# Edge stage of a graph network: the gathered rows are added on DVE instead of by an identity product on PE

## The reference

```python
def _L3_gnn_ref(h, edge_index, edge_attr, msg_w1, msg_b1, msg_w2, msg_b2, upd_w1, ...):
    src, dst = (edge_index[0], edge_index[1])
    m_in = jnp.concatenate([h[src], h[dst], edge_attr], axis=1)
    msg = jax.nn.relu(m_in @ msg_w1 + msg_b1) @ msg_w2 + msg_b2
    agg = jax.ops.segment_sum(msg, dst, num_segments=h.shape[0])
    upd_in = jnp.concatenate([h, agg], axis=1)
    upd = jax.nn.relu(upd_in @ upd_w1 + upd_b1) @ upd_w2 + upd_b2
    return h + upd
```

## Time and profile before

| | us |
|---|---|
| median of 3 runs | 3560.36 (3560.14 to 3565.21) |
| the profiled execution, its own time | 3566.42 |
| span of the profile | 3564.7 |
| mixed rounds of the edge stage, about | 2742 to 3503 |
| wide rounds | 3503 to 3548 |
| update of the nodes, the rest | 3548 to 3565 |

### The profile page before, as it was taken

The page is one execution under the profiler, slowest core; times in us unless marked ns, Lnnn a source line. Parts: engine busy times, 40 slices in busy tenths (PEclk is TensorE's granted clock), DMA queues, the critical chain, the costliest instruction groups (busy, mean ns, idle before and its releaser), DMA issues. The chain is left out here.

```text
span 3564.7 us, 82525 instructions
## 1 busy us (share of the span) xinstructions
PE 3252.6 (91%) x23698; PEld 2529.9 (71%) x23699; DVE 1620.1 (45%) x4433; ACT 1241.9 (35%) x3761; POOL 898.7 (25%) x938
## 2 busy tenths in 40 slices
PE   5988998989989989999789999999995999998988
PEld 3656666667764444444489999999884888888887
DVE  7977778889974320000544211111223443444444
ACT  6766777777751220000433222111332111111111
POOL 2000000000020000000067777000225656655550
PEclk8999999999999999999689999999997999999999
DMA  3012222333349378978044333222333434433431
GB/s 85 18 36 71 71 71 89 107 108 116 117 131 233 83 180 193 232 186 192 12 108 126 90 81 81 72 80 72 112 88 93 97 93 95 93 91 89 91 85 65
DMA packets 115781, 368.35 MB, mean 103 GB/s; under 512 B 37613, under 2 KB 54481, under 8 KB 102712
## 3 DMA queue, kind: packets, MB, share of 16 engines
q1 hardware_dynamic: 86647, 334.12, 34.0%
q0 software_dynamic: 25696, 29.21, 5.5%
q10 hardware_dynamic: 3154, 1.60, 0.2%
HBM read 278.22 MB, written 86.61 MB: 102 GB/s over the span
## 5 line engine op out<-in xcount | busy, mean ns | idle before, releaser
L2618 POOL DMA_INDIRECT edge_rows<-src_table,src_idx x432 | 460.5, 1066 | 307.0 <-DMA edge_rows<-src_table,src_idx 172.2
L2288 POOL DMA_INDIRECT slots<-lane,src_idx x352 | 342.1, 972 | 107.6 <-issue 107.6
L2828 ACT ACTIVATE edge_work<-edge_ps 128x1024 f32<-128x1024 f32 x114 | 116.7, 1023 | 702.7 <-PE edge_ps L2783 416.9
L1422 PE MATMUL prop_ps<-rows,y 125*128 125x500 f32 (+1 forms) x798 | 307.6, 545 | 15.2 <-DMA rows<-adj_rows 8.4
L781 ACT ACTIVATE build_place<-build_place,w 128x128 f32<-128x128 bf16 x690 | 265.0, 402 | 142.0 <-DVE build_place L725 101.6
L2797 PEld LDWEIGHTS edge_ps<-edge_work 128*128 128x128 f32 x2128 | 257.2, 195 | 65.7 <-issue 65.7
L851 PE MATMUL build_ps<-build_place 128*128 128x325 bf16 (+1 forms) x1380 | 299.0, 299 | 1.5 <-ACT build_place L781 0.4
L2797 PE MATMUL edge_ps<-edge_work 128*128 128x125 f32 x2128 | 266.2, 279 | 36.2 <-DVE m_agg_t L2667 36.2
L2773 PE MATMUL edge_ps<-m_store,edge_hot_t 125*128 x2128 | 272.3, 282 | 25.4 <-DVE edge_hot_t L2682 25.2
L2773 PEld LDWEIGHTS edge_ps<-m_store,edge_hot_t 125*128 125x128 f32 x2128 | 252.7, 195 | 35.8 <-issue 30.5
L1422 PEld LDWEIGHTS prop_ps<-rows,y 125*128 125x128 f32 x798 | 144.0, 192 | 176.9 <-issue 154.2
(11 more groups left out here) (462 smaller groups left out, 6205.9 us busy)
## 6 DMA issues: line engine op xcount, KB each, us to landing
rows<-adj_rows SPq DMA_DIRECT2D x62, 1367.2 KB
cnt_panels<-build_cnt SPq DMA_DIRECT2D x50, 683.6 KB
adj_rows<-rows SPq DMA_DIRECT2D x25, 1367.2 KB
n<-cnt_panels SPq DMA_DIRECT2D x40, 683.6 KB
orders_panel<-cnt_panels SPq DMA_DIRECT2D x40, 683.6 KB
edge_src_row<-slot_lanes SPq DMA_DIRECT2D x60, 250.0 KB
edge_dst_row<-slot_dst SPq DMA_DIRECT2D x60, 250.0 KB
h<-cnt_panels SPq DMA_DIRECT2D x20, 683.6 KB
```

The lines of the kernel that those rows point to most:

```text
L1422: last = pe.matmul(ps[:, c, 0:n * B], (y[0:B] if h else g.h)[:, row, 0:D], rows[slot][:, b0 * B:(b0 + n) * B], start=at == 0, stop=at == N ...
L2288: pool.indirect_dma_start(dr.slots, bass.IndirectOffsetOnAxis(ap=g.src_idx[:, j:j + 1], axis=0), g.pay[:, j, :], None).then_inc(s_scattere ...
L2618: pool.indirect_dma_start(rows[:, r % AHEAD, i, :], None, dr.table, bass.IndirectOffsetOnAxis(ap=g.src_idx[:, t:t + 1], axis=0)).then_inc( ...
L2828: a.activation(act[s], ps[:, 2 * s:2 * s + 2, :].rearrange("p b (t k) -> p (b t) k", k=D), ACT.Relu).then_inc(s_act[s], 1)
```

## The change

The identity product is left out. In its place DVE adds the gathered rows to slot 1's two banks and writes the result into `act[GATHERED]`, the messages' buffer (`join`); ACT takes the relu of that buffer in place. The last product of the edge values now ends `inputs` for a gathered group. A new semaphore `s_joined` lets ACT go on, and lets POOL reuse the buffer of the rows. ACT's loop is cut in two, one for the mixed rounds and one for the wide ones, whose work is as before.

```diff
--- before.py
+++ after.py
@@ -2523,6 +2523,7 @@
         s_free = [ph.sem(f"free{s}") for s in range(2)]
         s_pre = [ph.sem(f"pre{s}") for s in range(2)]
         s_act = [ph.sem(f"act{s}") for s in range(2)]
+        s_joined = ph.sem("joined")
         s_hot = ph.sem("hot")
         s_sum = ph.sem("sum")
         s_added = ph.sem("added")
@@ -2612,7 +2613,7 @@
                 if r:
                     pool.wait_ge(s_rows, r * (16 * GT))
                 if r >= AHEAD:
-                    pool.wait_ge(s_pre[GATHERED], r - AHEAD + 2)
+                    pool.wait_ge(s_joined, r - AHEAD + 1)
                 for i in range(GT):
                     t = SORTED + r * GT + i
                     pool.indirect_dma_start(rows[:, r % AHEAD, i, :], None, dr.table,
@@ -2667,12 +2668,24 @@
                 v.tensor_tensor(at, at, ps[:, bass.ds(bank + SUMS, 1), 0:B].rearrange("p a k -> p (a k)"),
                                 ALU.add).then_inc(s_added, 1)
 
-            def turned(r, s, wide):
+            def join(r):
+
+                here = v.snap(r & (AHEAD - 1), min_val=0, max_val=AHEAD - 1)
+                v.wait_ge(s_pre[GATHERED], r + 2)
+                v.wait_ge(s_rows, r * (16 * GT) + 16 * GT)
+                v.tensor_tensor(act[GATHERED].rearrange("p t k -> p (t k)"),
+                                ps[:, 2 * GATHERED:2 * GATHERED + 2, :].rearrange("p b k -> p (b k)"),
+                                rows[:, bass.ds(here, 1), :, :].rearrange("p o a k -> p (o a k)"),
+                                ALU.add).then_inc(s_joined, 1)
+
+            def turned(r, s, wide, joined=None):
 
                 load_range(v, regs, r, s)
                 if wide or s != GATHERED:
                     v.wait_ge(s_src[s], r * 16 + (16 if s != GATHERED else 16 - 16 * ROUNDS))
                     v.tensor_scalar(hot_s[s][0:B, :], src_row[s][:], lane[0:B, :], None, ALU.is_equal).then_inc(s_hot_s[s], 1)
+                if joined is not None:
+                    join(joined)
                 lo, end = limits_of(v, regs, s)
 
                 with v.Fori(lo, end) as d:
@@ -2704,7 +2717,7 @@
                 turned(r, 1, wide)
                 sums(r, 0, wide)
                 if not last:
-                    turned(r + 1, 0, wide)
+                    turned(r + 1, 0, wide, None if wide else r)
                 sums(r, 1, wide)
 
             turned(0, 0, False)
@@ -2754,6 +2767,10 @@
                                      a3.pq[0:B + 1, bass.ds(at[i], 1), 0, :].rearrange("p a k -> p (a k)"),
                                      start=i % 4 == 0, stop=False, skip_group_check=True)
 
+                def edge_value(i):
+                    return pe.matmul(place(s, i), ea_row[:, i * 128:(i + 1) * 128], a3.w_parts[:], start=i % 4 == 0,
+                                     stop=False, skip_group_check=True)
+
                 if sorted_group:
                     at = [pe.snap(reg, min_val=0, max_val=NB - 1) for reg in tiles]
                 pe.wait_ge(s_act[s], r + 1)
@@ -2763,9 +2780,8 @@
                     for i in range(GT - 1):
                         source(i)
                 else:
-                    for i in range(GT):
-                        pe.matmul(place(s, i), ea_row[:, i * 128:(i + 1) * 128], a3.w_parts[:], start=i % 4 == 0, stop=False,
-                                  skip_group_check=True)
+                    for i in range(GT - 1):
+                        edge_value(i)
                 with pe.Fori(lo, end) as d:
                     n = used[s].next()
                     pe.wait_ge(s_hot_t[s], n)
@@ -2777,12 +2793,7 @@
                 if sorted_group:
                     last = source(GT - 1)
                 else:
-                    here = pe.snap(r & (AHEAD - 1), min_val=0, max_val=AHEAD - 1)
-                    pe.wait_ge(s_rows, r * (16 * GT) + 16 * GT)
-                    for k in range(2):
-                        last = pe.matmul(ps[:, 2 * s + k, :], g.ident[:],
-                                         rows[:, bass.ds(here, 1), 4 * k:4 * k + 4, :].rearrange("p o a k -> p (o a k)"),
-                                         start=False, stop=True, skip_group_check=True)
+                    last = edge_value(GT - 1)
                 last.then_inc(s_pre[s], 1)
 
             def sums(r, s):
@@ -2822,11 +2833,18 @@
                 a.activation(dcol[:].rearrange("p (q c) -> p c q", c=PER_LOT)[:, 6 * i:6 * i + n, :],
                              ps[:, i, 0:n * LOTS].rearrange("p (c q) -> p c q", c=n), ACT.Copy).then_inc(s_dcol, 1)
             more = a.value_load(g.rounds[0:1, 0:1], min_val=1, max_val=MORE)
-            with a.Fori(0, a.snap(more + ROUNDS)) as r:
+            def taken(r, s):
+                a.wait_ge(s_pre[s], a.snap(r + 2))
+                a.activation(act[s], ps[:, 2 * s:2 * s + 2, :].rearrange("p b (t k) -> p (b t) k", k=D),
+                             ACT.Relu).then_inc(s_act[s], 1)
+
+            with a.Fori(0, ROUNDS) as r:
+                taken(r, 0)
+                a.wait_ge(s_joined, a.snap(r + 1))
+                a.activation(act[GATHERED], act[GATHERED], ACT.Relu).then_inc(s_act[GATHERED], 1)
+            with a.Fori(ROUNDS, a.snap(more + ROUNDS)) as r:
                 for s in range(2):
-                    a.wait_ge(s_pre[s], a.snap(r + 2))
-                    a.activation(act[s], ps[:, 2 * s:2 * s + 2, :].rearrange("p b (t k) -> p (b t) k", k=D),
-                                 ACT.Relu).then_inc(s_act[s], 1)
+                    taken(r, s)
 
 
 def update_phase(nc, g, a3, out):
```

## The result

The changed kernel took 3541.74 us (median of 6 runs, 3528.48 to 3550.18) against 3560.25 (median of 6, 3557.15 to 3568.53). The ratio is 0.9938, 95% interval 0.9912 to 0.9964: faster by some 22 us, with bounds of 13 and 31 (the two medians lie 18.5 us apart). The forecast was 3527.4 us with a range of 3500 to 3556. The profiled execution was the quickest of the six, 3528.48 us with a span of 3526.8.

A forecast was written before the change was run, and what follows sets the result against it. PE was taken to bound the mixed rounds, with POOL's gathers hidden some 30 us behind; of 93 us removed from PE, 33 were to show, so 3560.4 - 33 = 3527.4 us, range 3500 to 3556.

The forecast's parts named there:

- the 33 of the forecast: Mixed rounds: slot 0's hot_t matmuls of the last round start at 3474.0 instead of 3506.86 us, 33 of 93 us gained.
- the likeliest case: Whole kernel: the forecast of 3527.4 us, with its own range of 14 us either way, 3513 to 3541; chance 0.70.
- PE gains 1.72 us a round: PE, mixed rounds: removing the identity product saves 1.72 us in each of 54 rounds, 93 us in all.
- From then on DVE waits in the join for the rows: After about 17 mixed rounds DVE waits for gathered rows, PE for hot_t; gathers set the pace for the remaining 35.
- the five signs: No identity product; last gather near 3468; joins waiting in some 35 rounds; hot_t waits up 60 us; join 1.24 us.
- the distance between PE and POOL: Mixed rounds: gathered rows land some 25 to 30 us before PE uses them; PE can gain only some 30 us.
- The join: DVE, each mixed round: adding the gathered rows takes 1.24 us, hidden with 1.2 us to spare, costing nothing.
- ACT: ACT, mixed rounds: slot 1's relu from SBUF takes between 1.0 and 1.3 us and costs nothing.
- POOL: Gathers in mixed rounds: pace stays 14.2 us a group, landing and DVE effects taken to cancel.
- the rival of gathers slowed by it: POOL, mixed rounds: join delays each group's first gather by 1.24 us, giving 3570 or 3594 us; chance 0.08.
- The clock: PE's granted clock: no change was set for it, since rounds behind 3503 us already run at 84% with 1.00.
- The rival of the whole saving: Mixed rounds: gathers don't bind, so PE's full 93 us are saved, giving 3467 us; chance 0.02.

## Why the prediction came out right, and where it was wrong

The time fell into the range. The gain, 22 us with bounds of 13 and 31, lies below the 33 of the forecast, and the median of 3541.74 just outside the likeliest case's own 3513 to 3541. The mechanism behind the 33 was wrong, and two of its steps must be named.

*"PE gains 1.72 us a round"* is the step that failed. The product does go, and 1.72 us with it. But from sums to sources 0.86 us come back (1.79 to 2.65); the split of the eight small products costs 0.09 (0.49 + 0.15 against 0.55), and the `hot_t` products ahead of the last small one 0.09 (1.98 against 1.89). That leaves 0.68; measured at the full clock are 0.61. I had read the rows of PE's matmuls, in which nothing stood between sums and sources, and took the missing gap for slack. The order of PE's rows shows the register loads at that place; I cost them at nothing without naming what covers them. The cover was the very product that the change removes. Moving the two loads away brings the 0.8 us back, which is shown on two chips, and the same move gives nothing where the product still stands.

*"From then on DVE waits in the join for the rows"* never came. PE's 53 rounds got 23.6 us shorter (758.1 to 734.5), but the chain of gathers got shorter too: from its first start to its last end it takes 755.6 us instead of 767.1. So PE closed in on it by only 8 us over the whole stage: the landing lies 28.9 us ahead of its join in the first round and 20.6 in the last, with 5.8 as the least on the way. Three of the five signs that I had set for being right are missing. POOL's last gather ends at 3441.9 and not within 12 us of 3468 (15 us of this is its earlier start, the rest its pace). No join waits for a landing, though the list of waits names the gathers 19 times. PE's waits for `hot_t` grew by 2 us and not by 60. That the sum nevertheless met the measured gain is luck: the distance between PE and POOL (30 us) happens to be what 53 x 0.61 gives, and the half clock took 9 of it back (27 to 45 us), a term that I had set at nothing.

*The join* was sized right: 1224 ns against 1.24 us, and hidden as far as the runs can tell. *ACT*: 1057 ns, in the bounds of 1.0 and 1.3, hidden. *POOL*: its gathers took 1077 ns on the mean against 1066, and its pace was 13.99 us a group against 14.20, so the join did not hold it up, and the rival of gathers slowed by it is refuted. What the prediction's rows lacked is in the new trace: the 34 gathers that had a join and nothing else of DVE beside them took 943 ns on the mean, the 134 with DVE idle 944. The Trainium skill, "SBUF — State Buffer", on the shared port pair, says that a DVE instruction with at most one SBUF input, outside the two-port modes, does not contend with GpSimd. By that rule the join should leave the gathers alone, and the trace agrees. Why POOL's pace got 0.2 us a group quicker is open. *The clock*: the six executions of the changed kernel go from 3526.8 us of span at a clock of 0.971 to 3545.1 at 0.966 and 3548.4 at 0.967. That spread of 22 us is as large as the gain itself. The rival of the whole saving (3467 us) is as far off as it was said to be, though not for the reason given.

Against the kernel before on its own chip, the quickest version with all its gathers is the changed kernel with the tile numbers early: 0.9711 against 0.9825 on chip B, and in the pair with half the gathers 0.9167 against 0.9287 on chip C. On a chip with a high clock it was not run whole; there PE would come near the gathers, and part of its 0.8 us a round may stay out. That is open. Open is also why a chip holds the clock down in the mixed rounds when all rows are fetched and hardly when half are. The data hardly explain it: without the join no gathered row enters a message, and there were 362 us at half clock (on chip B; the halved gathers ran on C).

## What to carry to other kernels

Before an instruction of a long duration is taken off the busiest engine, look at what that engine's sequencer does right behind it: register loads, address arithmetic, loop ends. A gap of nothing between two groups of matmuls is no proof of slack; list the sequencer's rows there, add them up (here 2.5 us), and ask under which matmuls they lie. Of two chains of equal pace, read the distance between them group by group, after the change as well as before it. Measure both kernels between points that the change leaves at the same place of the round. And a wait for two semaphores must not be believed by name.

## What the runs showed of the hardware

- A load of one register pair from SBUF by PE's sequencer takes 540 ns, and one of four registers 332 ns (medians of 114 and 120). One of the first and two of the second with their arithmetic, 2.5 us, outlast 16 matmul passes (1.8 us from start to start).
- An add on DVE with one input in PSUM and one in SBUF, 128x1024 f32, does not lengthen an indirect gather's issue beside it: 943 ns (34 gathers) against 944 (134).
- The same program differs by 21% between chips: 3560 us on A and 4320 on C, mean granted clock 0.971 and 0.89. On B and C the mixed rounds had 261 to 362 us at half clock with all gathers (five kernels), and 41 to 58 with half of them (two, both on C); on D 31 to 48, all with half.
- On C time is lost beyond the half clock: with half of it taken off, the kernel before still needs 905 us where A needs 744. PE has 21 gaps of over 2.5 us there, 19 of them around a fall of the clock; the cause is open.
